# Router steps behind the sort: summing and one-input operations on VectorE, and small steps moved into ScalarE's copies

## What is computed

```
x = x + 0.5 * ffn(layernorm(x));  x = x + attn(layernorm(x));  x = x + 0.5 * ffn(layernorm(x))
# ffn: 8 experts (4 of width 128, 4 of width 256), the best 2 of them per token
probs = sigmoid(xf @ router_w.T)
topw, sel = top_k(probs, 2)
topw = topw / (topw.sum(-1) + 1e-20)
combine = sum(topw[:, :, None] * (sel[:, :, None] == arange(8)), axis=1)
h = square(relu(einsum('td,edw->tew', xf, W1e)))
out = einsum('ted,te->td', einsum('tew,ewd->ted', h, W2e), combine)
```

## Time and profile before

| | |
|---|---|
| runs of the kernel | 872.78 us median of 3 (869.69 to 877.11) |
| profiled execution, its own time | 871.08 us |
| its span, first to last instruction | 869.2 us |
| TensorE granted clock, mean of the span | 0.967 of full speed |
| busy share PE / DVE / ACT / POOL | 86% / 77% / 68% / 79% |
| matmuls; all instructions | 3648; 14035 |

### The profile page before, as it was taken

How to read it: one execution, slowest core, us unless ns; L and a number is a source line. 1 busy time by engine, 2 the same in 40 slices (tenths; PEclk the granted TensorE clock), 3 DMA queues, 4 the chain that set the end, 5 groups by cost and what they waited for, 6 DMA issues and landing times.

```text
span 869.2 us, 14035 instructions
## 1 busy us (share of the span) xinstructions
PE 750.6 (86%) x3648; PEld 600.7 (69%) x3648; DVE 669.3 (77%) x1882; ACT 587.3 (68%) x1187; POOL 686.5 (79%) x666
## 2 busy tenths in 40 slices
PE   1568778879999999989899998999999988987867
PEld 1446566657777787878677777878777876865645
DVE  4545679797989898998789897889889587586443
ACT  3447475758686877787586867777867765765645
POOL 3468677678899899999788997999989867666665
PEclk9899899999999999999999999999999999899899
DMA  5532122122332222232333330322323302302330
GB/s 164 170 123 83 64 97 63 37 98 99 98 98 98 70 82 76 95 110 98 112 98 110 98 108 20 116 76 98 109 99 110 110 7 92 110 20 91 110 109 24
DMA packets 21802, 79.32 MB, mean 91 GB/s; under 512 B 2272, under 2 KB 13280, under 8 KB 17632
## 3 DMA queue, kind: packets, MB, share of 16 engines
q1 hardware_dynamic: 19456, 76.03, 27.4%
q10 hardware_dynamic: 2272, 2.51, 0.9%
HBM read 73.81 MB, written 4.72 MB: 90 GB/s over the span
## 4 chain that ended last, share of the span: by engine, by line
PE 29%; DVE 22%; POOL 18%; issue 15%; DMA 8%; ACT 6%; POOLq 0%; DVEq 0%; ACTq 0%; SPq 0%
POOL h_lo L875 11%; DMA g_all_f<-rows_f 6%; DVE hid L1048 4%; PE bank L505 4%; PE bank L507 4%; PE bank L506 4%; PE bank L523 4%; PE bank L525 3%; PE bank L524 3%; POOL root_f L869 3%; DVE bn_f L944 2%; ACT h_hi L752 2%; ACT xn_f L702 2%; POOL x_lo_f L863 2%; PE bank L619 2%
## 5 line engine op out<-in xcount | busy, mean ns | idle before, releaser
L875 POOL TENSOR_TENSOR h_lo<-hid,h_hi 128x512 fp32r<-128x512 f32 x384 | 495.8, 1314 | 106.0 <-ACT h_hi L752 105.7
L1048 DVE SCALAR_TENSOR_TENSOR hid<-bank,g_all_f 128x512 f32<-128x512 f32 x384 | 261.7, 682 | 139.9 <-PE bank L507 77.1
L741 ACT ACTIVATE hid<-hid 128x512 f32<-128x512 f32 x384 | 229.8, 623 | 84.4 <-DVE hid L1048 82.0
L752 ACT ACTIVATE h_hi<-hid 128x512 fp32r<-128x512 f32 x384 | 225.7, 620 | 4.9 <-PE bank L525 0.4
L505 PE MATMUL bank<-x_hi_f,w_hi 128*128 128x512 f32 x384 | 170.2, 443 | 49.6 <-DVE hid L1048 42.6
L523 PE MATMUL bank<-h_hi,w_hi 128*128 128x512 f32 x384 | 157.1, 409 | 7.3 <-ACT yT L763 4.4
L506 PE MATMUL bank<-x_lo_f,w_hi 128*128 128x512 f32 x384 | 155.5, 405 | 0.0
L507 PE MATMUL bank<-x_hi_f,w_lo 128*128 128x512 f32 x384 | 155.5, 405 | 0.0
L525 PE MATMUL bank<-h_hi,w_lo 128*128 128x512 f32 x384 | 155.0, 404 | 0.0
L524 PE MATMUL bank<-h_lo,w_hi 128*128 128x512 f32 x384 | 154.8, 403 | 0.0
L505 PEld LDWEIGHTS bank<-x_hi_f,w_hi 128*128 128x128 f32 x384 | 75.0, 195 | 83.4 <-DVE hid L1048 55.9
(11 more groups left out here) (103 smaller groups left out, 1100.4 us busy)
## 6 DMA issues: line engine op xcount, KB each, us to landing
g_all_f<-rows_f SPq DMA_DIRECT2D x32, 1280.0 KB, 6.9
g_all_f<-rows_f SPq DMA_DIRECT2D x32, 768.0 KB, 8.4
x_sb<-in_x SPq DMA_DIRECT2D x16, 256.0 KB, 3.8
out_x<-x_sb SPq DMA_DIRECT2D x16, 256.0 KB, 8.5
g_all_f<-in_w ACTq DMA_DIRECT2D x2, 768.0 KB, 7.2
con<-in_const ACTq DMA_DIRECT2D x1, 652.0 KB, 7.0
rows_f<-g_row_f SPq DMA_DIRECT2D x32, 16.0 KB, 1.4
g_all_f<-in_wqkv ACTq DMA_DIRECT2D x1, 192.0 KB, 9.4
```

The source lines that it names most:

```text
L741: fn(h, h, ACT.Square).then_inc(s_sq[s], 1)
L752: fn(h_hi[:, c, :], hid[:, c % STAGE, :], ACT.Copy).then_inc(s_hhi[s], 1)
L875: gp.tensor_tensor(h_lo[:, c, :], hid[:, c % STAGE, :], h_hi[:, c, :].bitcast(F32), ALU.subtract).then_inc(s_hlo[s], 1)
L1048: v.scalar_tensor_tensor(hid[:, c % STAGE, :], hp[c % 2][:], 0.0, g_all[s][:, EXPERT[c], :], ALU.max, ALU.mult).then_inc(s_z[s], 1)
```

## The change

On ACT: `exp_logits` gets a second activation, `odds` = 1 x ex + 1 (L733 of the kernel after), in place of DVE's `tensor_scalar`; the copy to `g_row` becomes Relu(g - 2e-19), which makes a root below 2e-19 zero, as `g_top`'s mask did; the copy `yT` of the FFN's output gets the scale 0.5, and the "x 2" is gone. On DVE: `best` gets a column in front that holds 1e-20, and `tot` is one `tensor_reduce` over three columns in place of a `tensor_tensor` and a `tensor_scalar`; `cwt` also writes an accumulator (`cw_sum`, not read by anything); `g_top` is gone, `pick` reads the root itself; `g_tok` is a `tensor_reduce` over the two picks. The steps also stand at other places on DVE:

| step (DVE) | f1: behind place, before -> after | f2 |
|---|---|---|
| 1 + exp | 3 -> ACT | 15 -> ACT |
| reciprocal (`prob`) | 4 -> 4 | 16 -> 16 |
| max | 7 -> 5 | 19 -> 17 |
| max_index, `tot` | 8 -> 6 | 20 -> 18 |
| `rtot` | 11 -> 6 | 23 -> 18 |
| `cw`, `cwt` | 11, 11 -> 7, 8 | 23, 23 -> 19, 20 |
| `chosen` | 10 -> 10 | 22 -> 21 |
| `g_top` | 12 -> none | 0 -> none |
| `pick` | 13 -> 11 | 1 -> 0 |
| `g_tok` | 14 -> 12 | 2 -> 1 |

POOL's and PE's orders are as before, apart from two memsets on POOL at the start.

The diff, cut to the functions:

```diff
@@ act.exp_logits
                 fn(ex[s][:], l, ACT.Exp, scale=-1.0).then_inc(s_ex[s], 1)
+                if due(n):
+                    act.wait_ge(s_prob[s], value(n))
+                act.wait_ge(s_ex[s], value(n + 1))
+                fn(odds[s][:], ex[s][:], ACT.Identity, bias=c_one[:, 0:1]).then_inc(s_odds[s], 1)
@@ act.rows_of_weights, copy_yT
-                fn(g_row[s][:], tp[0:EXP * TG, 0:P], ACT.Copy).then_inc(s_gr[s], 1)
+                fn(g_row[s][:], tp[0:EXP * TG, 0:P], ACT.Relu, bias=c_cut[0:EXP * TG, 0:1]).then_inc(s_gr[s], 1)
-                fn(yT[:], yp[s][:], ACT.Copy).then_inc(s_yT[s], 1)
+                fn(yT[:], yp[s][:], ACT.Copy, scale=0.5).then_inc(s_yT[s], 1)
@@ pool.root_of_weights
-                pool.wait_ge(s_cw[s], value(n * 3 + 3))
+                pool.wait_ge(s_cwt[s], value(n + 1))
@@ dve.pick_two -> where_two
-                    v.tensor_tensor(tot[s][:], best[s][:, :, 0], best[s][:, :, 1], ALU.add).then_inc(s_rt[s], 1)
...
-                    v.tensor_scalar(tot[s][:], tot[s][:], 1e-20, 2.0, ALU.add, ALU.mult).then_inc(s_rt[s], 1)
+                v.tensor_reduce(tot[s][:], best[s][:, :, 0:1 + TOPK], AX.X, ALU.add).then_inc(s_tot[s], 1)
@@ dve.weigh_two
-                    v.tensor_scalar(cwt[s][:], cw[s][:], TINY, None, ALU.max).then_inc(s_cw[s], 1)
+                    v.tensor_scalar(cwt[s][:], cw[s][:], TINY, 0.0, ALU.max, ALU.add, accum_out=cw_sum[s][:]) \
+                        .then_inc(s_cwt[s], 1)
@@ dve.spread_roots
-                    v.scalar_tensor_tensor(g_top[s][:], cw[s][:], 0.0, root[s][:], ALU.is_gt, ALU.mult) \
-                        .then_inc(s_gm[s], 1)
...
+                    dve.wait_ge(s_root[s], value(n + 1))
+                    dve.wait_ge(s_chosen[s], value(n + 1))
+                    v.tensor_tensor(pick[s][:], chosen[s][:], root[s][:].unsqueeze(3).to_broadcast([P, TG, TOPK, EXP]),
+                                    ALU.mult).then_inc(s_pick[s], 1)
...
-                    v.tensor_tensor(g_tok[s][:].rearrange("p e k -> p k e"), pick[s][:, :, 0], pick[s][:, :, 1], ALU.add) \
-                        .then_inc(s_gt[s], 1)
+                    v.tensor_reduce(g_tok[s][:].rearrange("p e k -> p k e"), pick[s][:].rearrange("p k i e -> p k e i"),
+                                    AX.X, ALU.add).then_inc(s_gt[s], 1)
@@ dve.iteration, f1
-                pick_two("f1", n1, 3)
+                choose_two("f1", n1)
                 weighted(t, 11)
-                weigh_two("f1", n1, 0)
-                weigh_two("f1", n1, 1)
-                weigh_two("f1", n1, 2)
+                spread_roots("f1", n1, 0)
                 weighted(t, 12)
                 high_part("f2", n2, p2)
-                spread_roots("f1", n1, 0)
+                spread_roots("f1", n1, 1)
                 weighted(t, 13)
-                spread_roots("f1", n1, 1)
```

More of the change, by code:

```diff
@@ L57 @@
 TINY = 1.2e-38
+ROOT_CUT = 2e-19
 KVW = D + HEADS
@@ L252, in build @@
         root = {s: sb(f"root_{s}", [P, TG, TOPK]) for s in FFN}
-        g_top = {s: sb(f"g_top_{s}", [P, TG, TOPK]) for s in FFN}
-        c_half = sb("c_half", [P, TG, TOPK])
+        c_half, c_one, c_cut = sb("c_half", [P, TG, TOPK]), sb("c_one", [P, 1]), sb("c_cut", [P, 1])
+        cw_sum = {s: sb(f"cw_sum_{s}", [P, 1]) for s in FFN}
         yT = sb("yT", [P, NTOK])
@@ L315, in build @@
         s_ex = per("ex", FFN)
-        s_rt = per("rt", FFN)
+        s_odds = per("odds", FFN)
+        s_prob = per("prob", FFN)
+        s_best = per("best", FFN)
+        s_which = per("which", FFN)
+        s_tot = per("tot", FFN)
+        s_rtot = per("rtot", FFN)
+        s_cw = per("cw", FFN)
+        s_cwt = per("cwt", FFN)
         s_chosen = per("chosen", FFN)
-        s_cw = per("cw", FFN)
         s_root = per("root", FFN)
-        s_gm = per("gm", FFN)
+        s_pick = per("pick", FFN)
         s_gt = per("gt", FFN)
@@ new lines, in where_two @@
+                dve.wait_ge(s_best[s], value(n + 1))
+                dve.sem_inc(s_gate, 1)
+                v.tensor_reduce(tot[s][:], best[s][:, :, 0:1 + TOPK], AX.X, ALU.add).then_inc(s_tot[s], 1)
+                for k in range(TG):
+                    i = v.max_index(which[s][:, k, :], best[s][:, k, 1:], prob[s][:, k, :])
+                i.then_inc(s_which[s], 1)
+                dve.wait_ge(s_tot[s], value(n + 1))
+                v.reciprocal(rtot[s][:], tot[s][:]).then_inc(s_rtot[s], 1)
@@ L1004, in weigh_two, with choose_two @@
                 if step == 0:
[L1005 to L1006 removed]
+                    dve.wait_ge(s_rtot[s], value(n + 1))
+                    v.tensor_tensor(cw[s][:], best[s][:, :, 1:1 + TOPK], rtot[s][:].unsqueeze(2).to_broadcast([P, TG, TOPK]),
+                                    ALU.mult).then_inc(s_cw[s], 1)
                 elif step == 1:
[L1008 to L1013 removed]
+                    dve.wait_ge(s_cw[s], value(n + 1))
+                    v.tensor_scalar(cwt[s][:], cw[s][:], TINY, 0.0, ALU.max, ALU.add, accum_out=cw_sum[s][:]) \
+                        .then_inc(s_cwt[s], 1)
+            def choose_two(s, n):
+                if not live(n):
+                    return
+                dve.wait_ge(s_which[s], value(n + 1))
+                v.tensor_tensor(chosen[s][:], which[s][:, :, 0:TOPK].unsqueeze(3).to_broadcast([P, TG, TOPK, EXP]),
+                                expert, ALU.is_equal).then_inc(s_chosen[s], 1)
             def spread_roots(s, n, step):
```

92 lines of the change are left out of this document (32 added, 60 removed).

## The result

The changed kernel takes 902.4 us (median of 4 runs, 900.4 to 909.4) beside 874.9 of the kernel before on the same chip: 1.034 times as long, interval 1.026 to 1.041. The forecast was slower, 889 us, with 902 as the upper end, so the sign was right and the time lies just above the range. The kernel before had 872.8 when the forecast was made and has 874.9 here, so the rise is 27.5 us where 16 were forecast. The profiled execution took 901.66 us with a span of 899.6, which is 30.4 more than before. 1.7 of these are no part of the change: PE's first instruction, which waits for the first input, starts at 13.24 us here and at 11.50 in the trace before. Every trace of this case has one of these two starts (11.5 to 11.6, or 13.1 to 13.4), with old code and new.

A forecast was written before the change was run, and what follows sets the result against it. PE was taken as the bound, with stops waiting for DVE. Per middle iteration +2.9 - 0.8 - 1.4 + 1.2 = +1.9, ten times +19, with -1.7 and -1 +16: 872.8 + 16 = 889 us; own range 880 to 900, whole range 866 to 902.

The forecast's parts named there:

- new stop at place 14: PE's up of place 14 waits for the hid of place 12: mean +2.9 us per middle iteration, bounds 1.7 and 3.4.
- lower clock: PE's matmuls slow down after the new gap: 1.7 us in seven of ten iterations, mean +1.2, bounds 0 and 1.7.
- relief of DVE: About 4.9 us less DVE per iteration, cutting PE's stops by 0.8 us before L619 and 1.4 at places 23 and 0.
- up to the first middle iteration: Start, where no chunk covers the router: 1 + exp on ACT shortens the chain, 1.7 us less, bounds 0 and 2.9.
- f2's side of the end: The f2 side of the last iterations: 1 us less, bounds 0 and -4.
- The added wait: On DVE, pick waits for POOL's unchanged root of f1 ahead of place 12's hid, making place 14's up 3.4 us later.
- the clock holds: Rival: all as forecast but without the 1.2 us per iteration of lower clock, 877 us; chance 14%.
- Start and ends: Outside the middle: 1.7 us less at the start, nothing for later one-stream waits, 1 less on f2's last iterations.
- The one-stream stretches: Where one stream runs, g_tok comes two places sooner but pick holds place 12's hid: taken as 0, bounds -8 and +6.
- the relief doesn't come: Rival: POOL holds cw, chosen and pick in full, stops at L619 and place 0 stay: +4.8 per iteration, 919 us; 7%.

The follow-up runs named there:

- the stops filled: Changed kernel plus eleven result-neutral matmuls on PE ahead of f2's up of place 13 while f1 has work: 893.7 us, ratio 1.024 to the kernel before.
- first experiment: Changed kernel with f1's pick back behind the hid of place 12 and its g_tok behind that of place 13: 856.4 us, ratio 0.984 to the kernel before.
- the early root: Changed kernel with POOL's root of f1 moved ahead of the remainders of places 6 and 7: 845.1 us, ratio 0.972 to the kernel before.

## Why the prediction was right in sign and too small

The forecast's terms for ten middle iterations and the ends, beside what the traces have:

| Term | forecast | measured |
|---|---|---|
| new stop at place 14 (PE's idle time there) | +29 | +28.9 |
| lower clock (PE's busy time) | +12 | +12.0 |
| relief of DVE (the rest of PE's idle time) | -22 | -11.4 |
| longer stops behind the loop's jumps | none | +3.5 |
| up to the first middle iteration | -1.7 | -1.7 |
| f2's side of the end | -1 | -0.3 |
| sum | +16 | +31 (span +30.4) |

- **The added wait: right.** PE's idle time at place 14 is 3.3 to 3.4 us in six of ten iterations and 2.2 in four, mean 2.89 (forecast 3.4 and 2.4, mean 2.9; the expectations above count 0.16 more for each, 3.05). Its parts were right too: DVE idle ahead of `pick`, `pick` 1.27 us, the root no earlier than POOL's list lets it, although `cwt` was there 8 us sooner. The runs with this wait alone (+42.3 in the middle) and without it (856.4) show it from both sides.
- **The clock: the mechanism right, the size in part by luck.** With the stops filled, 9 us of the middle came back, and the iterations with no jump, but for the first, ran at a clock of 1.00. But of the 31 us more that the changed kernel spends at the lower clock only 20 go with the stops at place 14. The other 10 lie behind the jumps: before, the clock was low there for 3.4 us in all, with the stops filled for 13.6, and no term of the forecast had this. The rival "the clock holds" is out.
- **The relief: the step that failed.** The forecast had 2.2 us less of stops in each iteration, 0.8 before the attention product ("so it goes") and 1.4 at places 23 and 0; about half of it came. The stop at place 23 went; the idle time before the product fell from 0.68 to 0.37 us only, that at place 0 from 0.83 to 0.32. The first error is a mean. Ahead of the product the forecast took off `g_top` at 834 ns, the mean of all 32. The `g_top` that stands there is f2's, and the trace before had it at 0.17 us in every middle iteration; only f1's took 1.24. By its means `g_top`, 1 + exp and half of `g_tok` make 1.6 us; by the rows that stand there (0.17, 0.17 and 0.71 for a whole `g_tok`, which became 0.21) the change takes 0.84 away:

```profile
333.19 0.17 DVE L1021 SCALAR_TENSOR_TENSOR g_top_f<-cw_f,root_f 128x8 f32<-128x8 f32 x1
...
334.07 0.89 DVE L1026 TENSOR_TENSOR pick_f<-chosen_f,g_top_f 128x64 f32<-128x64 f32 x1
```

  The second is what came back on other instructions. The changed and removed steps take 57 us less over the ten iterations (61 forecast), but the others take some 18 more where 12 were booked, and not on `cw`, where they were booked (+3.1): `pick` +6.6, `chosen` +6.1, the rounding of x for the FFNs +4.7, `kf` +4.2, with `qf` 4.7 less. So DVE's work fell by 3.9 us per iteration, not 4.9. The third is two waits that took the place of work. DVE's own rows of the changed kernel at the start of an iteration:

```profile
335.31 1.06 DVE L1119 SCALAR_TENSOR_TENSOR kf<-kb,ka 128x512 f32<-128x512 f32 x1 [0.79 <-ACT kb L783]
...
337.91 1.31 DVE L1036 TENSOR_TENSOR pick_f<-chosen_f,root_f 128x64 f32<-128x64 f32 x1 [0.60 <-POOL root_f L881]
```

  Before, `rtot`, `cw` and `cwt` stood between the sum of k and `kf` and covered ScalarE's exp; with them gone `kf` waits 0.79 us for it (0.29 before), and `pick` of f2, which had `g_top` ahead of it and took 0.89 us, now waits for its root and is held for 1.31 us. From `kf` to `kvm` DVE needs 9.19 us where it needed 9.44. This reading is of the traces; the runs that moved f2's root and chosen gained only 0.2 us per ordinary iteration, so it isn't shown that these two waits carry all of the shortfall, and how it divides stays open.
- **What no term had: the jumps.** In the two iterations behind a jump PE's stop is 1.9 and 1.7 us longer, 3.5 together. Where the stop at place 14 is taken out (first experiment), eight ordinary iterations gain 11.5 us against before and these two lose 3.1. The price of a loop's jump was taken as fixed; it changes with the code.
- **Start and ends: right in number, by luck.** PE waits 7.0 us for its first `g_tok`, not 8.86. But the first input came 1.7 us later in this execution, so with an equal start the way to the middle got 3.4 us shorter, twice the forecast. The one-stream stretches were booked at nothing; `pick` blocked them: without the block the middle starts 4.6 us earlier still (180.80), and with the early root 13 at an equal start (170.54).

Of the rivals, "the relief doesn't come" (919 us, 7%) was the nearest in kind: half of the relief did not.

## What to carry to other kernels

When an instruction that waits for a slow engine is moved forward in an in-order queue, read where the thing it waits for stands in the other engine's queue: an input that is ready earlier brings nothing as long as the consumer's list is unchanged. Here moving the producer on POOL as well turned +3.4% into -2.8%. And work that is removed from an engine is worth only what is not already covering a wait of its own: look at what the next instruction waits for before the gain is booked. A step is priced at the rows of the place where it stands: a mean over 32 of them was 834 ns here, and the one on the path took 0.17 us.

## What the runs showed of the hardware that was not expected

- Code position has a price: sixteen idle instructions at the program's start, with nothing else changed, took about 1 us off the time from the loop's jump to DVE's second instruction at three of four jumps. Between the kernel before and the changed one this time grew by 2.4 us (3.4 to 3.5, then 5.7 to 6.0); there the loop's code differs too, so how much of it is position isn't shown.
- A pause of PE of 3.4 us is paid for a second time through the clock (51.2 us for an iteration, 48.6 with the pause filled), and useless matmuls in it made the kernel about 1% faster. The length of the pause doesn't settle it: behind stops of 2.06 us with the root one instruction earlier the clock fell in three of four ordinary iterations (0.69 over 348 to 352), and behind one of 3.32 us in the changed kernel it stayed at 1.00.
- Sums over 12 and 64 elements take 156 and 212 ns beside a busy POOL, while a product of two operands in SBUF with 64 results takes 1.27 us there and 0.22 us when POOL is idle. The form decides, not the size, and not the number of inputs alone: `cwt` has one input, and as a plain `tensor_scalar` it took 631 ns on average, with an accumulator 204.
